# Self loops as 8-column products behind each quarter, and a group's eight sums on two halves of the matmul columns, in two tables

## The reference, cut to what matters

```python
ft = (hn @ W_att).reshape(n, H, DH)
scores = jnp.einsum('ehd,ehd->eh', ft[src], ft[dst]) / jnp.sqrt(jnp.float32(DH))
m = jax.ops.segment_max(scores, dst, num_segments=n)
ex = jnp.exp(scores - m[dst])
z = jax.ops.segment_sum(ex, dst, num_segments=n)
agg = jax.ops.segment_sum(ft[src] * (ex / z[dst])[:, :, None], dst, num_segments=n)
```

```python
deg = jax.ops.segment_sum(jnp.ones_like(d), d, num_segments=n_nodes)
norm = dis[s] * dis[d]                      # dis = rsqrt(deg)
out = jax.ops.segment_sum(h[s] * norm[:, None], d, num_segments=n_nodes) + b
```

## Time and profile before

| what | value |
|---|---|
| device time, median of 3 runs | 3986.43 us (3984.04 to 3987.22) |
| the profiled execution: span from its first to its last instruction | 3987.6 us |
| PE matmul busy | 3679.6 us, 92% of the span |
| DVE busy | 2167.3 us, 54% |
| ACT busy | 1880.8 us, 47% |
| POOL busy | 1505.2 us, 38% |
| instructions | 61,840 |

### The profile page before, as it was taken

One profiled execution on the slowest core, in us unless ns is written; L12 is line 12 of the kernel. 1 busy time (PEld: TensorE's weight loads), 2 busy tenths in 40 slices (PEclk: granted clock), 3 DMA queues, 4 the chain that ended last, 5 costly groups with the idle time before them and its releaser, 6 DMA issues. The chain is left out here.

```text
span 3987.6 us, 61840 instructions
## 1 busy us (share of the span) xinstructions
PE 3679.6 (92%) x21902; PEld 2157.9 (54%) x21902; DVE 2167.3 (54%) x3396; ACT 1880.8 (47%) x5147; POOL 1505.2 (38%) x1605
## 2 busy tenths in 40 slices
PE   5899999999999999999985879999999999999999
PEld 3566666666666666666653544445444544454444
DVE  8788888888888888888874750002100210012000
ACT  4788888888888888888863660002000100011000
POOL 2677777777777777777760000000000000000000
PEclk8788888888888888888886989999999999999999
DMA  6443333333333333333334126665666566665665
GB/s 202 128 109 104 105 106 105 105 106 105 106 105 105 106 106 106 105 106 105 105 92 88 38 65 204 204 196 181 199 194 208 174 194 203 205 189 184 213 204 159
DMA packets 467250, 560.45 MB, mean 141 GB/s; under 512 B 45449, under 2 KB 411684, under 8 KB 466686
## 3 DMA queue, kind: packets, MB, share of 16 engines
q1 hardware_dynamic: 383558, 366.63, 30.4%
q0 software_dynamic: 51168, 107.68, 12.2%
q10 hardware_dynamic: 32248, 82.62, 5.6%
HBM read 455.16 MB, written 103.20 MB: 140 GB/s over the span
## 5 line engine op out<-in xcount | busy, mean ns | idle before, releaser
L900 POOL DMA_INDIRECT fts<-ft_tab,src_all x1568 | 1483.0, 946 | 478.0 <-issue 477.4
L2171 PE MATMUL cv_acc<-cv_cnt,cv_parts 128*128 128x512 bf16 (+1 forms) x7056 | 1431.3, 366 | 0.0
L2171 PEld LDWEIGHTS cv_acc<-cv_cnt,cv_parts 128*128 128x128 bf16 x7056 | 666.0, 98 | 761.7
L2006 DVE TENSOR_TENSOR cv_y<-cv_acc,dis_row 128x512 f32<-128x512 f32 (+1 forms) x52 | 34.4, 661 | 1355.1 <-PE cv_acc L2171 1326.5
L937 DVE TENSOR_TENSOR ohk<-iota_ps,key_cols 128x784 bf16<-128x784 f32 x784 | 724.9, 966 | 6.1
L1030 ACT ACTIVATE dist_l<-lo_iota,low 128x128 bf16<-128x128 f16 x1960 | 593.7, 388 | 18.6 <-ACT low L1025 0.8
L1189 PE MATMUL agg_ps<-terms,oh 128*64 128x141 f32 x2744 | 528.7, 364 | 25.6 <-DVE terms L974 25.0
L1189 PEld LDWEIGHTS agg_ps<-terms,oh 128*64 128x64 f32 x2744 | 458.1, 180 | 80.6 <-DVE terms L974 67.3
L1082 ACT CAST strip<-adj_ps 128x392 bf16<-128x392 f32 x784 | 372.2, 475 | 271.4 <-PE adj_ps L1133 239.2
L1133 PE MATMUL adj_ps<-ohk,ohl 128*128 128x196 bf16 x3136 | 431.2, 263 | 0.0
L951 DVE TENSOR_TENSOR prod<-ftd_ps,fts 128x780 f32<-128x780 f32 (+1 forms) x392 | 271.1, 692 | 220.5 <-DMA fts<-ft_tab,src_all 212.3
(11 more groups left out here) (261 smaller groups left out, 2919.9 us busy)
## 6 DMA issues: line engine op xcount, KB each, us to landing
cv_cnt<-adj SPq DMA_DIRECT2D x96, 2048.0 KB, 8.3
cv_cnt<-adj SPq DMA_DIRECT2D x48, 2176.0 KB, 8.6
adj<-strip ACTq DMA_DIRECT2D x196, 392.0 KB
fts<-ft_tab,src_all POOLq DMA_INDIRECT x1568
win<-ft_tab SPq DMA_DIRECT2D x196, 65.0 KB
agg_tab<-res SPq DMA_DIRECT2D x196, 35.2 KB
cv_cnt<-adj SPq DMA_DIRECT2D x8, 512.0 KB, 3.7
agg_tab<-zero_f SPq DMA_DIRECT2D x10, 352.5 KB
```

The costliest lines, as they stand in the source:

```text
L900: nc.gpsimd.indirect_dma_start(fts[u][:, k, :], None, ft_tab[:, :], bass.IndirectOffsetOnAxis(src_all[:, n, k:k + 1], 0)).then_inc(gathere ...
L2171: last = nc.tensor.matmul(a[:, 0:width], parts[:, r, b, :], cnt[q][:, 0:width // SUB, (b - b0) * SUB:(b - b0 + 1) * SUB], start=(b == 0 an ...
```

## The change

**Self loops.** In each quarter of `count` the product of 392 columns ahead of the four one-hot products is gone. Behind them comes a product of `ident_bf` (128 x 128) by 8 columns of `ident_bf`, written with stride to the 8 columns of the diagonal. The tiles `own` and `own_low`, and what fills them, go too.

**Sums.** Column n of a group is added to PSUM partitions 64 to 127 where n is even and to 0 to 63 where it is odd (`side_of`). So `res`, `fade`, `move` and `shared` have 128 partitions, each store becomes two DMAs into two tables, and `agg_tab` has two tables: twenty writes of zeros in the prelude, and fourteen loads in `normalise`, where DVE adds the two before anything else, and ACT waits for the last addition.

**The turned row.** Its old place is now in use, so it goes to the free ends of the two banks of `ftd_ps`, by two products of 64 columns in place of one of 128; `highest` reads both. On DVE `highest` now stands ahead of `first_products`.

Left out below are changed shapes of the small tiles, the semaphores' counts that follow from the doubled DMAs, and the removal of the unused iota `row_no`.

```diff
@@ -78,7 +78,7 @@
     row_tab = dram("row_tab", (NG, 4, 512), FP16)
-    agg_tab = dram("agg_tab", (TAB, WA), F32)
+    agg_tab = dram("agg_tab", (2, TAB, WA), F32)
     edge_score = dram("edge_score", (EX, H), F32)
@@ -353,8 +351,10 @@
             for k in range(10):
-                sp.dma_start(agg_tab.rearrange("(p b) w -> p b w", p=P)[:, k * (TAB // P // 10):(k + 1) * (TAB // P // 10), :]
-                             .rearrange("p b w -> p (b w)"), zero_f[:]).then_inc(s["pads_out"], 16)
+                for side in range(2):
+                    sp.dma_start(agg_tab[side].rearrange("(p b) w -> p b w", p=P)
+                                 [:, k * (TAB // P // 10):(k + 1) * (TAB // P // 10), :]
+                                 .rearrange("p b w -> p (b w)"), zero_f[:]).then_inc(s["pads_out"], 16)
             sp.wait_ge(s["keys_made"], 1)
@@ -534,7 +534,7 @@
                 dve.wait_ge(s["base_summed"], 1)
-                nc.vector.tensor_scalar(shared[:], base_ps[0:WD, 0:NG], row_no[0:WD, :], None, ALU.is_equal)
+                nc.vector.tensor_scalar(shared[:], base_ps[:, 0:NG], float(MID), place[:], ALU.subtract, ALU.is_equal)
                 nc.vector.tensor_tensor(irr_part[:], irr_part[:], base_ps[0:1, NG:NG + 1], ALU.add)
@@ -770,13 +770,11 @@
         shift = sb("shift", [P, 2, 2], F32, c)
-        fade = sb("fade", [WD, 2, 2], F32, c)
-        move = sb("move", [WD, 2, 2], F32, c)
+        fade = sb("fade", [P, 2, 2], F32, c)
+        move = sb("move", [P, 2, 2], F32, c)
         terms = sb("terms", [P, 2, GC, WA], F32, c)
-        res = sb("res", [WD, UN, WA], F32, c)
+        res = sb("res", [P, UN, WA], F32, c)
         iota_sb = sb("iota_sb", [P, KEYS + P], F32, c)
-        own = sb("own", [SUB, NA, 2 * KEYS], BF16, c)
-        own_low = sb("own_low", [SUB, 2 * P - SUB], BF16, c)
         lo_iota = sb("lo_iota", [P, P], FP16, c)
@@ -822,8 +819,11 @@
 
+        def side_of(column):
+            return agg_ps[(1 - column % 2) * WD:(2 - column % 2) * WD, 0:WA]
+
         def turned_row(k):
-            return agg_ps[WD:WD + 1, 0:P]
+            return ftd_ps[0:1, :, (HC - 1) * HD:(HC - 1) * HD + P // 2]
 
@@ -837,8 +837,9 @@
                 if n:
-                    sp.wait_ge(agg_out, 16 * n)
-                sp.dma_start(agg_tab[ds(base, WD), :], res[:, n % UN, :]).then_inc(agg_out, 16)
+                    sp.wait_ge(agg_out, 32 * n)
+                for side in range(2):
+                    sp.dma_start(agg_tab[side, ds(base, WD), :], res[side * WD:(side + 1) * WD, n % UN, :]).then_inc(agg_out, 16)
 
@@ -908,13 +909,7 @@
             nc.vector.memset(fade[:], 1.0).then_inc(consts, 1)
-            nc.vector.memset(own[:], 0.0).then_inc(own_made, 1)
-            nc.vector.memset(own_low[:], 0.0).then_inc(own_made, 1)
             nc.vector.memset(hr_3[:], 0.0).then_inc(rest_zero, 1)
-            dve.wait_ge(own_made, 2)
-            nc.vector.tensor_copy(own[:, :, KEYS:KEYS + HALF], ident_bf[0:SUB, 0:SUB].rearrange("p (a d) -> p a d", d=HALF)
-                                  ).then_inc(own_made, 1)
-            nc.vector.tensor_copy(own_low[:, P - SUB:P], ident_bf[0:SUB, 0:SUB]).then_inc(own_made, 1)
             for s in range(2):
@@ -943,7 +938,7 @@
                     dve.wait_ge(spread, k.n - 1)
-                nc.vector.tensor_reduce(most[:, k.s:k.s + 1], turned_row(k), AX.X, ALU.max).then_inc(most_done, 1)
+                nc.vector.tensor_reduce(most[:, k.s:k.s + 1], turned_row(k), AX.XY, ALU.max).then_inc(most_done, 1)
 
@@ -999,10 +994,10 @@
                     key_one_hots(k, 2)
+                if two.exists():
+                    highest(two)
                 if one.exists():
                     first_products(one)
-                if two.exists():
-                    highest(two)
                 if k.exists():
@@ -1073,8 +1068,8 @@
                 if k.after(UN):
-                    act.wait_ge(agg_out, 16 * (k.n - UN + 1))
-                nc.scalar.copy(res[:, k.u, :], agg_ps[0:WD, 0:WA]).then_inc(res_done, 1)
+                    act.wait_ge(agg_out, 32 * (k.n - UN + 1))
+                nc.scalar.copy(res[:, k.u, :], agg_ps[:, 0:WA]).then_inc(res_done, 1)
 
@@ -1125,13 +1120,16 @@
                     pe.wait_ge(strip_done, 4 * k.n + q - 1)
-                tile_of = own[:, q * QS:(q + 1) * QS, KEYS - HALF * k.j:2 * KEYS - HALF * k.j]
-                nc.tensor.matmul(adj_ps[q % 2][:, 0:QS * KEYS], own_low[:, P - SUB - SUB * k.u:2 * P - SUB - SUB * k.u], tile_of, start=True, stop=False)
+                counts_ps = adj_ps[q % 2][:, 0:QS * KEYS]
                 for a in range(QS):
...
                         n = q * QC + a * SC + m
-                        last = nc.tensor.matmul(adj_ps[q % 2][:, a * KEYS:(a + 1) * KEYS], ohl[:, k.s, n, :],
-                                                ohk[:, k.s, n, :], start=False, stop=(a == QS - 1 and m == SC - 1))
+                        nc.tensor.matmul(counts_ps[:, a * KEYS:(a + 1) * KEYS], ohl[:, k.s, n, :], ohk[:, k.s, n, :],
+                                         start=(a == 0 and m == 0), stop=False)
+                first = SUB * k.u + q * QS * HALF
+                last = nc.tensor.matmul(counts_ps.rearrange("p (a t d) -> p a t d", a=QS, d=HALF)[:, :, k.j, :], ident_bf[:],
+                                        ident_bf[:, first:first + QS * HALF].rearrange("p (a d) -> p a d", d=HALF),
+                                        start=False, stop=True)
                 last.then_inc(adj_done, 1)
@@ -1180,14 +1178,16 @@
                     pe.wait_ge(most_done, k.n)
-                nc.tensor.matmul(turned_row(k), score[:, k.at(1).c, GC * H:GC * H + 1], ident[:],
-                                 start=True, stop=True).then_inc(turned, 1)
+                for a in range(2):
+                    last = nc.tensor.matmul(turned_row(k)[:, a, :], score[:, k.at(1).c, GC * H:GC * H + 1],
+                                            ident[:, a * P // 2:(a + 1) * P // 2], start=True, stop=True)
+                last.then_inc(turned, 1)
 
...
                     half, col = divmod(n, HC)
-                    nc.tensor.matmul(agg_ps[0:WD, 0:WA], oh[:, k.o, col, half, :], terms[:, k.s, n, :],
-                                     start=(n == 0), stop=False)
+                    nc.tensor.matmul(side_of(n), oh[:, k.o, col, half, :], terms[:, k.s, n, :],
+                                     start=(n < 2), stop=(n == GC - 2))
 
@@ -1210,7 +1210,7 @@
             def last_sum(k):
-                nc.tensor.matmul(agg_ps[0:WD, 0:WA], oh[:, k.o, HC - 1, 1, :], terms[:, k.s, GC - 1, :],
+                nc.tensor.matmul(side_of(GC - 1), oh[:, k.o, HC - 1, 1, :], terms[:, k.s, GC - 1, :],
                                  start=False, stop=True).then_inc(agg_done, 1)
@@ -1257,14 +1256,18 @@
         odd_n = sb("no_odd_n", [P, 1], F32, c)
+        other = sb("no_other", [P, NT, WA], F32, c)
         odd_ps = pb("no_odd_ps", [P, 512], F32, c)
         raw_in = [sem(f"no_raw_in{k}") for k in range(NB)]
-        chain, marked, rooted, odd_made, odd_sum = (sem("no_" + s) for s in (
-            "chain", "marked", "rooted", "odd_made", "odd_sum"))
+        chain, joined, marked, rooted, odd_made, odd_sum = (sem("no_" + s) for s in (
+            "chain", "joined", "marked", "rooted", "odd_made", "odd_sum"))
         block = c.enter_context(nc.Block())
-        load = lambda engine, k: engine.dma_start(
-            raw[:, k * BATCH:(k + 1) * BATCH, :],
-            agg_tab[k * BW:(k + 1) * BW, :].rearrange("(b p) w -> p b w", p=P)).then_inc(raw_in[k], 16)
+
+        def load(engine, k):
+            for side, to in enumerate((raw, other)):
+                engine.dma_start(to[:, k * BATCH:(k + 1) * BATCH, :],
+                                 agg_tab[side, k * BW:(k + 1) * BW, :].rearrange("(b p) w -> p b w", p=P)
+                                 ).then_inc(raw_in[k], 16)
 
@@ -1276,7 +1279,9 @@
                 b = slice(k * BATCH, (k + 1) * BATCH)
-                dve.wait_ge(raw_in[k], 16)
+                dve.wait_ge(raw_in[k], 32)
+                nc.vector.tensor_tensor(raw[:, b, :], raw[:, b, :], other[:, b, :], ALU.add).then_inc(joined, 1)
+                dve.wait_ge(joined, k + 1)
                 nc.vector.scalar_tensor_tensor(odd[:, b, 0:H], raw[:, b, HD:HD + H], FAINT,
@@ -1299,8 +1304,7 @@
                 load(act, k)
-            for k in range(NB):
-                act.wait_ge(raw_in[k], 16)
+            act.wait_ge(joined, NB)
             nc.scalar.activation(root[:], raw[:, :, WA - 1], ACT.Sqrt, bias=1.0).then_inc(rooted, 1)
```

More of the change, by code:

```diff
@@ L142, in gnn_program @@
             g["low_cols"] = sb("low_cols", [P, NG, NA, SC], F32, lists)
-            g["shared"] = sb("shared", [WD, NG], F32, lists)
+            g["shared"] = sb("shared", [P, NG], F32, lists)
             g["spots"] = sb("spots", [5, P], FP16, lists)
@@ L232, in prelude @@
         place = sb("place", [P, 1], F32, c)
-        row_no = sb("row_no", [P, 1], F32, c)
```

(13 more changed lines are left out.)

## The result

The changed kernel takes 3998.93 us (median of 10 runs, 3992.55 to 4001.42), the kernel before measured beside it 3985.56 us (10 runs, 3983.14 to 3989.26). The ratio is 1.0032, with a 95% interval of 1.0023 to 1.0040: slower by 0.32%. The forecast was 3997.5 us. The profiled execution of the changed kernel has a span of 3997.0 us, against 3987.6 before.

The account below looks back on a forecast made before the run. POOL's own gather issue was taken to bound the attention loop, at 10.0 us a group. Terms 0 + 1.7 - 3.8 + 13.2 = +11.1 us on 3986.4 gave 3997.5 us, own range 3993 to 4003, stated range 3990 to 4005.

Parts of the forecast that it names:

- Loop, 0 us: Attention while it gathers: POOL's gathers keep 10.0 us a group, so PE's saved time becomes waiting; 0 us.
- a DVE wait for gathers well above 212 us: Sign of a right forecast, in the attention's loop: DVE waits for gathers to land well above the earlier 212 us.
- DVE's 8.7 us a group: Attention loop, inside the half-clock rival: groups not bound by PE can't go below DVE's 8.7 us.
- Prelude, +1.7 us: Prelude: ten more zero writes delay the keys' write 3.5 us, less 1.75 slack; +1.7 us (0 to +5).
- The low end of my range: Prelude: 0 us, if the queue lets the keys overtake the zeros or there is slack further on.
- The attention's end, -3.8 us: After the last gather: `highest` -0.3, alternating sums -4.35, split turn +0.3, second store +0.55; -3.8 us (-5.3 to +1.2).
- the features' 139 ns: Time per record of destination features alternating between row halves at half clock, scaled to forecast the end's sums at 2.1 us.
- The rival that the sums do not overlap: Attention's end: three groups of sums keep 3.55 us each; +4.35 us, total 4001.9 us; 18 in 100.
- Normalise, +13.2 us: Normalise: twice the bytes loaded at 291 GB/s, +12.1 us, and the last addition, +1.1; +13.2 us (+5 to +15).
- The rival of loads at 386 GB/s: Normalise: loads move at 386 GB/s, taking 18.3 us, not 24.2; total +5.2, 3991.6 us; 12 in 100.
- The clock's rival: Attention loop: PE stays at half clock and becomes the bound in nearly all groups; +437 us, 4430 us; 6 in 100.

Follow-up runs that it names:

- The self loops alone: The kernel before with only the 8-column self-loop products and nothing else of the change: 3986.43 us against 3986.36, ratio 1.0001.
- The runs with six gathers: Kernel before and changed kernel, each leaving out two of a group's eight gathers after the first six groups (stale rows): 3810.2 us (0.9562) and 3813.47 us (0.9564).

## Why the prediction was right, step by step

**Loop, 0 us: right.** The self loops alone gave 1.0001, the gathers' spacing is the same in both kernels, and removing gathers, not PE's work, shortened the loop. One sign came only faintly: I had asked for a DVE wait for gathers well above 212 us, and it was 235 and 224 in the two profiles of the changed kernel, 212 and 204 before; PE's own waits took the rest. I had DVE's 8.7 us a group only as a floor in a rival. The runs with six gathers point to DVE right behind POOL, so that PE's saving had little worth in a loop with a faster POOL too.

**Prelude, +1.7 us: right in mechanism, a little low.** I had the fetch 3.5 us later and 1.75 of slack. It came 4.0 later, the second turn 3.9, and DVE's store of the keys 2.2, so the slack was right and the delay some 0.4 too small. Half of that was in my own sum: from about 47 us to 50.7 are 3.7 us and not 3.5. At the first gather, the four profiles without the second zeros average 117.9 us (117.3 to 118.5) and the five with them ahead of the keys 120.2 (119.6 to 121.5): +2.3. The low end of my range, a queue that lets the keys overtake or more slack further on, did not come. To take the loss back the writes had to be put where the DMA engines have room. Just behind the keys they have none.

**The attention's end, -3.8 us: right at the half clock, a little less over several executions.** The alternating sums took 2.14 us where I had scaled 2.1 from the features' 139 ns, so three groups gave 4.2 (4.35 forecast). The second store cost 0.62 (0.55 forecast), and the way from the first products to the first sums is 0.44 shorter (0.3 forecast, for `highest`). The split turn, which I had at +0.3, cost 0.01: 0.59 us against 0.58 at the same half clock. With PE at the half clock throughout, the end fell from 25.6 to 21.3 and 21.4 us, by 4.2. But in other executions PE had the full clock for part of the end: 23.0 and 23.3 us where the sums use one half, 20.1 in three of the kernels that alternate (their second group's sums took 1.17, 1.17 and 1.39 us), a gain of 3.0. Over all, three profiles with sums on one half average 24.0 and six with alternating sums and two tables 20.7, so -3.2 here. What was missed: I took the half clock of one execution for the kernel's.

The Trainium skill, "TensorEngine Tiling (Array Packing)", Key Properties, states that different tiles can work at the same time. The trace agrees: 14 records in 2.14 us, which is 0.60 of the serial 3.55. The rival that the sums do not overlap is thereby out.

**Normalise, +13.2 us: right.** It grew by 12.7 and 12.8 us: 11.6 for the reads (12.1 forecast), 1.2 for the last addition (1.1 forecast). Leaving the second read and the additions out gave all of it back. The rival of loads at 386 GB/s fails: the loads ran at 300 to 309 GB/s with the DMA share at 1.15. By its own sum that rival would have decided from about 335 GB/s on, not from 325; the loads reached neither. The reads' term is 0.5 us below the forecast, about what a rate of 300 in place of 291 GB/s gives (7.08 MB then take 23.6 us, 11.5 more than the 12.1 of before).

**The clock's rival: out.** Over the attention the granted clock fell from 0.86 to 0.79, but no wait of POOL came of it beyond the one of 0.3 us. PE was busy 81% of the time even so.

**The sum.** Prelude +2.3, loop 0, end -3.2 on the average of the profiles, normalise +12.8: +11.9 us. The medians lie 13.4 apart in the first comparison and 13.3 in the last. The 1.4 us between lie inside the interval of the ratio (0.0009 of 3986 is 3.6 us to either side) and no section accounts for them. Against the profiles the forecast of +11.1 was 0.6 too low in the prelude, 0.6 too high in the end's gain and 0.4 too high in normalise. Against the times it was 2.3 us too low. That 3997.5 lies only 1.4 from the measured 3998.93 is in part luck: it started from 3986.4, and beside the changed kernel the kernel before took 3985.56.

## What to carry to other kernels

Work taken off an engine that is busy 92% of a stretch is worth nothing when another engine's queue sets the pace; the row that decides is what ended the idle time of the pacing engine, here 1568 times its own issue. Doubling a table to save engine time is paid in bytes wherever the table is written and read, and the stages where nothing else runs pay it in full: here 3.5 MB more of reads cost 11.6 us. When a delayed transfer is moved, look at what the DMA engines carry just where it goes; behind the keys it only moved the wait, between the batches it was free.

## What the runs showed of the hardware

- Two levels of an execution: the gathers of the same kernel were 1.2507 us apart in one execution and 1.2483 in another, 3.8 us over 1567 of them, and the eleven profiles with eight gathers a group lie at 1.2483 to 1.2487 (nine) or at 1.2504 and 1.2507 (two). The cause is open. Single traces can't be compared below that.
- Sums in f32 on alternate halves of the columns: 2.14 us for 14 records of 141 columns at the half clock, against 3.55 on one half. In two blocks, one for each half, they took 2.67.
- The same idle times ahead of the same three groups of sums left PE at 0.5 of the clock in one execution and let it rise in another, by the length of the sums (3.55, 3.55, 3.55 us and 3.55, 2.91, 2.46). From the second to the third group the granted clock was 0.50 in the one and 0.83 in the other, in the stretch between their sums.
- The stretch behind normalise varied from 1860.9 to 1864.6 us over the profiles, though no kernel differs there.
